# Three regroupings in a transformer-block kernel: order of the first loads, the last group's weight sums, and the first expert's W2

## The chip, the cores and the metric

The kernel runs on one core of one Trainium2 chip. The metric is the device time of one execution, in microseconds (us). Three runs of the kernel before gave 2044.21, 2045.13 and 2047.85 us; the median is 2045.13 us. TensorE is called PE here, VectorE DVE, ScalarE ACT, GpSimd POOL, SyncE SP, as in the profile.

## What is computed

One block of a perceiver over 16 batches of 128 query rows (`x`, 16 x 128 x 512) and 2048 context rows (`ctx`, 16 x 2048 x 512), all float32:

```python
x = x + xattn(layernorm(x), ctx, ctx, ...)      # 16 heads of 32, one shared K and V head
x = x + memory(layernorm(x), Ww, Wr, decay, log_alpha)   # chunks of 64, a 64x64 inverse per chunk and head
x = x + ffn(layernorm(x), Wg, w1, w2)           # 16 experts, top-1, capacity 128 rows each
```

Attention is softmax(Q K^T / sqrt(32)) V, then Wo. The memory layer projects v = x Ww^T, normalizes x per head to rk, inverts (I - A0) per chunk, forms the chunk's new values from v, reads them out with rk and projects with Wr^T. The FFN sends each row to the expert with the largest gate (at most 128 rows an expert, in order), computes relu(rows w1) w2 and multiplies by the gate.

## The kernel before

**Two stages.** `attention` does cross attention, the memory layer and the routing for 16 batches (b = 0 to 15, `LAST` = 15) and scatters each batch's rows to the dispatch table in DRAM. `experts` then takes the 16 experts one after the other, with the weights of the next one loaded meanwhile (two buffers of w1, two of w2, 4 MB each). Between the two stages all engines meet at the end of a block.

**The order of the work** is written out by hand. Every engine runs the same loop over batches and over 128 ticks a batch, and tables of ticks (`FIRST`, `SECOND`, `STEADY`, `PE_AT`, `ACT_AT`, `DVE_AT`, `POOL_AT`) say at which tick a step's instructions stand in that engine's program. So a tick sets only an order; waits on semaphores set the times. `prepare` makes batch b+1's queries, keys and values while batch b attends; `finish` runs batch b-1's projection, memory layer and routing in the same loop.

**Attention of a batch** has 4 groups of 4 heads. For each group PE computes the scores twice: once to find the row maxima on DVE (L425, `largest`), once transposed with the maximum subtracted (L438, `score`), 16 tiles of 128 keys. ACT exponentiates each tile into one of 18 buffers `p` (the tensor `weights`, L673). PE multiplies them with the values, four 32-column strips of the array at once (L450, `weigh`), and POOL adds the 16 tiles of a group elementwise into `psum` (even tiles) and `podd` (odd ones), L1053, and at the end the two into one, L1056 (`add_weights`). `sums` (L459 to L473) then sums over the 128 keys of the partitions with a matrix of ones, into KV_BANK, one strip of 32 output rows for each group, and adds up the outputs `oS` in P_BANK in the same way. DVE takes reciprocals (L900).

**The start.** SP loads the identity, Wq and the context chunks 1 to 3 of batch 0 (L329 to L332); ACT, at the head of its own program, loads the biases, x, Wk/Wv (`wkv`) and context chunk 0 (L662 to L665). Each of these two engines has a DMA queue of its own. PE projects chunk c with 8 matmuls of 32 columns (L507), in the order chunk 0, the transposes of x (L390), 4 filler matmuls (L642), chunk 1, the query projection (L492), chunk 2, the transposes of the first half of the keys and values, chunk 3, then the first scores (L425). The query, split into a high and a low part, is sent to its place by 12 small DMAs (`send_queries`, L340).

**The last batch** has nothing to run beside it: only its chain of dependent steps is left, from the last exponential to the scatter of its rows. PE is kept busy there with filler matmuls on zeros (`busy`, L454). The steps that the change touches, in PE's order: filler, `sums`, filler, the output projection `x1` in T_BANK, filler, transposes of xn2 (L390), filler, the four matmuls of the value projection V (L394 with `ww`), filler, transposes of rk, filler, rk times rk (`I`, L398), filler, transposes of XT (`X1`), and then six levels of the inverse. All but x1 go through P_BANK, and ACT copies each result out. `V` is first used after the inverse (`Vn`, L588).

**Counts.** Semaphores are counted by name: `Named` turns a step's name and its batch into the value to wait for, so a change of order needs a change of the names' order.

## Time and profile before

| | us |
|---|---|
| median of 3 runs (2044.21 to 2047.85) | 2045.13 |
| the profiled execution, its own time | 2050.84 |
| its span, first to last instruction | 2048.7 |
| PE busy in the span | 1978.4 (97%) |
| POOL busy | 1618.7 (79%) |
| DVE busy | 1287.9 (63%) |
| ACT busy | 1094.3 (53%) |
| mean granted PE clock | 0.982 of full |
| bytes moved by DMA | 262.21 MB, mean 128 GB/s |

Stages by the clock of the span: the first 160 us are a ramp in which PE has gaps; from there to about 1555 us batches follow one another; 1555 to 1622 us is the chain of the last batch; 1622 to 2048 us are the experts. A granted clock of 1.00 is the higher of PE's two levels (2.4 GHz), 0.50 the lower (1.2 GHz); a value between them is a stretch with some of each. PE's float32 matmuls are recorded as two instructions each, so x8 in a row of the trace is four matmuls of the program.

### The profile page before, as it was taken

The page shows a single profiled execution, that of the slowest core. Times are in us where ns is not written, and L with a number is a line of the kernel's source. Part 1 is how long each engine was busy: PE and PEld are TensorE (multiplying, and loading weights), DVE is VectorE, ACT ScalarE, POOL GpSimd, SP SyncE. Part 2 cuts the span into 40 slices and gives each one's busy share as a digit, 9 for nine tenths or more (in the row PEclk, how much of TensorE's full clock was granted, in tenths as well). Part 3 has the DMA queues.
Part 4 walks back from the last instruction along what each step waited for, and adds up shares of the span by engine and source line. Part 5 has one row for each costly group of instructions (what it writes and reads, how often), then busy time and mean ns, then how long its engine had stood idle before and what let it go on. Part 6 is the DMA issues. An engine that isn't in the chain of part 4 may idle for free. (4 is left out here: it accounts for less than half of the span.)

```text
span 2048.7 us, 34177 instructions
## 1 busy us (share of the span) xinstructions
PE 1978.4 (97%) x12396; PEld 1304.4 (64%) x12396; DVE 1287.9 (63%) x2218; ACT 1094.3 (53%) x2029; POOL 1618.7 (79%) x1387
## 2 busy tenths in 40 slices
PE   6889999999999999999999999999999899999998
PEld 3435565656565555556565556555556799999998
DVE  4776868677777768686877767686852333333333
ACT  2555665665656656666656566565553233333333
POOL 0778999998999999999999999999895155555555
PEclk7889999999999999999999999999999999999999
DMA  5434231212122221312121212211200399999994
GB/s 214 171 113 121 88 102 47 78 47 78 47 78 69 67 76 54 98 52 82 46 78 45 78 66 68 68 56 25 98 1 17 119 359 358 356 356 356 352 364 170
DMA packets 105127, 262.21 MB, mean 128 GB/s; under 512 B 8576, under 2 KB 33920, under 8 KB 96256
## 3 DMA queue, kind: packets, MB, share of 16 engines
q1 hardware_dynamic: 96336, 234.66, 33.2%
q10 hardware_dynamic: 5040, 14.88, 1.9%
q0 software_dynamic: 3584, 10.49, 1.3%
q8 instruction: 99, 1.62, 0.3%
q14 instruction: 68, 0.56, 0.1%
HBM read 223.67 MB, written 25.72 MB: 122 GB/s over the span
## 5 line engine op out<-in xcount | busy, mean ns | idle before, releaser
L848 DVE TENSOR_REDUCE mpart<-bank 128x1 f32<-128x512 f32 x1024 | 662.6, 682 | 239.2 <-PE bank L425 233.6
L673 ACT ACTIVATE weights<-bank 128x512 f32<-128x512 f32 x1024 | 581.9, 598 | 306.4 <-PE bank L438 304.7
L1053 POOL TENSOR_TENSOR podd<-podd,weights 128x512 f32<-128x512 f32 x384 | 495.1, 1289 | 32.5 <-ACT weights L673 31.6
L1053 POOL TENSOR_TENSOR psum<-psum,weights 128x512 f32<-128x512 f32 x384 | 503.6, 1311 | 2.6 <-ACT weights L673 1.6
L438 PE MATMUL bank<-qT,kT 97*128 97x512 f32 x1024 | 477.6, 473 | 5.7 <-DMA qT<-mrow 3.8
L425 PE MATMUL bank<-kT,qT 96*128 96x512 f32 x1024 | 426.5, 441 | 7.5 <-DVE mpart L848 5.9
L425 PEld LDWEIGHTS bank<-kT,qT 96*128 96x128 f32 x1024 | 195.5, 193 | 145.5 <-DVE mpart L848 110.9
L450 PE MATMUL bank<-weights,v 128*32 128x512 f32 x2048 | 274.8, 609 | 0.0
L438 PEld LDWEIGHTS bank<-qT,kT 97*128 97x128 f32 x1024 | 198.0, 194 | 110.0 <-ACT weights L673 51.1
L1309 POOL TENSOR_TENSOR w2l<-w,w2h 128x1024 fp32r<-128x1024 f32 x64 | 202.9, 3171 | 76.9 <-PE ebank L1222 56.1
L1252 ACT ACTIVATE hh<-ebank 128x512 fp32r<-128x512 f32 x64 | 38.2, 597 | 226.0 <-PE ebank L1206 226.0
L1246 ACT CAST w2h<-w 128x2048 fp32r<-128x2048 f32 x64 | 121.4, 1898 | 43.7 <-DMA w<-in_w 43.7
L507 PE MATMUL bank<-w_first,wkv 128*32 128x512 f32 x1024 | 127.1, 615 | 11.9 <-DMA w_first<-in_ctx 8.5
L1278 DVE SCALAR_TENSOR_TENSOR hl<-ebank,hh 128x512 fp32r<-128x512 f32 x64 | 44.2, 691 | 133.7 <-ACT hh L1252 133.7
L1273 DVE TENSOR_TENSOR w2l<-w,w2h 128x1024 fp32r<-128x1024 f32 x64 | 79.3, 1239 | 72.3 <-PE ebank L1222 49.6
L1206 PE MATMUL ebank<-dT,w_first 128*128 128x128 f32 x1024 | 118.3, 275 | 0.9 <-DVE dT L1267 0.9
L1206 PEld LDWEIGHTS ebank<-dT,w_first 128*128 128x128 f32 x1024 | 117.3, 192 | 2.4 <-issue 1.2
L1206 PEld LDWEIGHTS ebank<-dT,w 128*128 128x128 f32 x1024 | 117.5, 192 | 1.4
L1206 PE MATMUL ebank<-dT,w 128*128 128x128 f32 x1024 | 118.2, 275 | 0.0
L944 DVE TENSOR_TENSOR xr<-xr,bank 128x512 f32<-128x512 f32 (+2 forms) x114 | 62.9, 562 | 82.4 <-PE bank L398 80.1
L1220 PE MATMUL ebank<-w2h,hh 128*128 128x512 f32 x256 | 104.9, 410 | 1.9 <-POOL w2l L1309 1.9
L398 PEld LDWEIGHTS bank<-xr,Y 128*128 128x128 f32 x640 | 78.5, 191 | 43.4 <-DVE Y L930 30.8
(171 smaller groups left out, 2995.1 us busy)
## 6 DMA issues: line engine op xcount, KB each, us to landing
w<-in_w SPq DMA_DIRECT2D x48, 2048.0 KB, 20.1
w_first<-in_ctx SPq DMA_DIRECT2D x63, 1024.0 KB, 4.9
w_first<-in_w SPq DMA_DIRECT2D x16, 2048.0 KB, 11.7
dispatched<-route ACTq DMA_DIRECT2D x17, 513.0 KB, 4.2
dis<-dispatched SPq DMA_DIRECT2D x16, 513.0 KB, 3.5
qT<-qh SPq DMA_DIRECT2D x124, 64.0 KB, 2.1
qT<-qs SPq DMA_DIRECT2D x64, 64.0 KB, 2.1
xr<-in_x SPq DMA_DIRECT2D x16, 256.0 KB, 2.7
```

The lines of the kernel that those rows point to most:

```text
L425: e.matmul(a[:], qT[b % 2][0:3 * HD, (4 * g + h) * P:(4 * g + h + 1) * P], kT[b % 2][0:3 * HD, c * 512:(c + 1) * 512], start=True, stop=Tr ...
L438: e.matmul(B_BANK[u % 2][:], kT[b % 2][0:3 * HD + 1, k * P:(k + 1) * P], qT[b % 2][0:3 * HD + 1, g * 512:(g + 1) * 512], start=True, stop= ...
L450: ins = e.matmul(PV_BANK[HD * j:HD * (j + 1), :], v1[b % 2][:, k + j, :], p[(UNITS * b + u + j) % NP], start=k == 0, stop=k == KB - 4)
L507: ins = e.matmul(KV_BANK[row:row + HD, :], wkv[:, j, n:n + HD], cxT[c][:, j, :], start=j < 2, stop=j >= 2)
L673: e.activation(p[n % NP], B_BANK[u % 2][:], ACT.Exp).then_inc(p_act.sem, 1)
L848: e.tensor_reduce(mpart[g % 2][:, 4 * (n % 4) + n // 4:4 * (n % 4) + n // 4 + 1], max_bank(b, g, n)[:], AX.X, ALU.max).then_inc(max_dve.se ...
L1053: e.tensor_tensor(acc[:], first, p[(UNITS * b + u) % NP], ALU.add).then_inc(psum_pool.sem, 1)
L1206: ins = e.matmul(H_BANK[g][:, f * P:(f + 1) * P], w1[q][:, c, (4 * g + f) * P:(4 * g + f + 1) * P], dT[q][:, c, :], start=c == 0, stop=c = ...
L1220: e.matmul(Y_BANK[q][:], hh[g % 2][:, part], w2h[g][:, f, :], start=k == 0, stop=False)
L1246: e.copy(w2h[g][:], w2[q][:, 4 * g:4 * g + 4, :]).then_inc(w2h_act.sem, 1)
L1273: e.tensor_tensor(w2l[g % 2][:, 0:2, :], w2[x % 2][:, 4 * g:4 * g + 2, :], w2h[g][:, 0:2, :].bitcast(F32), ALU.subtract).then_inc(w2l_dve. ...
L1309: e.tensor_tensor(w2l[g % 2][:, 2:4, :], w2[q][:, 4 * g + 2:4 * g + 4, :], w2h[g][:, 2:4, :].bitcast(F32), ALU.subtract).then_inc(w2l_pool ...
```

## The change

Four edits.

1. **First loads.** SP now loads x, Wk/Wv, context chunk 0, Wq and chunks 1, 2, 3, in this order. ACT loads only the identity and the biases. In `FIRST`, batch 0's chunks 2 and 3 get earlier ticks, with the steps that follow from them, and the first row maximum too.
2. **Sums of the last group.** For the last batch's last group POOL adds only tiles 2 to 9 (`DIRECT` = 10). PE sums `psum`, `podd` and the six tiles 10 to 15 into the fourth strip of KV_BANK.
3. **Values of the last batch.** The V projection of the last batch moves behind `I` and goes to T_BANK; the transposes of rk no longer wait for it.
4. **W2 of expert 0.** The buffer `weights` becomes expert 0's (and every second expert's) w2 buffer; SP loads W2 of expert 0 as soon as `sums` of the last batch is done, in the attention stage, and no longer at the start of the expert stage.

```diff
-FIRST = Prep(norm=4, norm_pool=4, xn=6, xnt=8, xnt_act=8, qproj=[11, 12, 13, 40], q_dve=15, q_act=16, q_pool=18,
-             qsend=19, kv=[7, 10, 40, 62], kvlow=[7, 10, 16, 71], kvs=[8, 11, 17, 34], kh=[9, 12, 64, 89], kl=[11,
-             14, 51, 64], vt=[53, 67], vt_act=[76, 125])
+FIRST = Prep(norm=4, norm_pool=4, xn=6, xnt=8, xnt_act=8, qproj=[11, 12, 13, 14], q_dve=15, q_act=16, q_pool=18,
+             qsend=19, kv=[7, 10, 16, 18], kvlow=[7, 10, 16, 31], kvs=[8, 11, 17, 22], kh=[9, 12, 18, 37], kl=[11,
+             14, 20, 64], vt=[20, 67], vt_act=[20, 73])
+PE_LAST = dict(PE_AT, rkT=PE_AT["V"][0], I=PE_AT["V"][1], V=[PE_AT["X1"] - n for n in (4, 3, 2, 1)])
+ACT_LAST = dict(ACT_AT, rkT=ACT_AT["rk"] + 1, V=ACT_AT["X1"])
...
         @block.sync
-            e.dma_start(ident, T["consts"][:, C_IDENT, :]).then_inc(ident_in.sem, 16)
+            e.dma_start(xin[:], T["x"][0]).then_inc(x_in.sem, 16)
+            e.dma_start(wkv[:], T["Wkv"]).then_inc(wkv_in.sem, 16)
+            load_ctx(0, 0)
             weight(e, wq[:], "Wq").then_inc(wq_in.sem, 16)
             for c in (1, 2, 3):
                 load_ctx(0, c)
...
+                    if t == W2_AT and i == B:
+                        e.wait_ge(*sums_pe.at(LAST))
+                        for j in (0, 1):
+                            load_w2(e, T, weights, 0, j).then_inc(w2_in[j].sem, 16)
...
             def sums(b):
-                e.wait_ge(*psum_pool.at(b, 15 * HG - 1))
-                e.wait_ge(*oS_act.at(b, HG - 1))
+                e.wait_ge(*psum_pool.at(b, 15 * HG - 1 if b < LAST else 15 * (HG - 1) + DIRECT - 3))
+                if b < LAST:
+                    e.wait_ge(*oS_act.at(b, HG - 1))
...
+                sources = [[psum[(HG * b + g) % 5][:]] for g in range(HG)]
+                if b == LAST:
+                    sources[3] += [podd[:]] + [p[(UNITS * b + 3 * KB + k) % NP] for k in range(DIRECT, KB)]
+                for n in range(len(sources[3])):
+                    if b == LAST and n >= 2:
+                        e.wait_ge(*p_act.at(b, 3 * KB + DIRECT + n - 2))
                     for g in range(HG):
-                        ins = e.matmul(out[HD * g:HD * (g + 1), :], lhs, src[g][:], start=True, stop=True)
+                        if n < len(sources[g]):
+                            ins = e.matmul(KV_BANK[HD * g:HD * (g + 1), :], cst[:, C_ONES, 0:HD], sources[g][n],
+                                           start=n == 0, stop=n == len(sources[g]) - 1)
...
                 if t == PE_AT["rkT"]:
-                    e.wait_ge(*post_act.at(b, "V"))
+                    e.wait_ge(*post_act.at(b, "V" if b < LAST else "xn2T"))
                     e.wait_ge(*post_act.at(b, "rk3"))
...
         @block.scalar
+            e.dma_start(ident, T["consts"][:, C_IDENT, :]).then_inc(ident_in.sem, 16)
             e.dma_start(bias[:], T["bias"]).then_inc(bias_in.sem, 16)
-            e.dma_start(xin[:], T["x"][0]).then_inc(x_in.sem, 16)
-            e.dma_start(wkv[:], T["Wkv"]).then_inc(wkv_in.sem, 16)
-            e.dma_start(cxT[0], T["ctx"][0, 0]).then_inc(ctx_in[0].sem, 16)
...
             def add_weights(b, u):
-                if k < 2:
+                if k < 2 or (b == LAST and g == 3 and k >= DIRECT):
                     return
...
 def experts(nc, T, w1_first, w1_in_first, w2_first, w2_in_first):
-                    e.dma_start(w2[q][:, 8 * j:8 * j + 8, :], T["w2"][x].rearrange(
-                        "(h c p) m -> h p c m", p=P, h=2)[j]).then_inc(w2_in[q][j].sem, 16)
+                    if x:
+                        load_w2(e, T, w2[q], x, j).then_inc(w2_in[q][j].sem, 16)
```

How the instructions stand, at three places (the order of each engine's program, without times). First PE in the last batch, from the filler ahead of `sums` to the output projection (psum, podd, weights, oS: what is summed; mneg: the filler). Before:

```order
L457 MATMUL bank<-mneg 124x124 x8
L472 MATMUL bank<-psum,cst 32x512 x4
L472 MATMUL bank<-oS,cst 32x512 x4
L457 MATMUL bank<-mneg 124x124 x11
L394 MATMUL bank<-wo,turned 128x512
```

and with the change:

```order
L474 MATMUL bank<-mneg 124x124 x8
L495 MATMUL bank<-psum,cst 32x512 x4
L495 MATMUL bank<-podd,cst 32x512
L495 MATMUL bank<-weights,cst 32x512 x6
L500 MATMUL bank<-oS,cst 32x512 x4
L474 MATMUL bank<-mneg 124x124 x11
L411 MATMUL bank<-wo,turned 128x512
```

Seven matmuls are added, all for the fourth group, between those of `psum` and those of `oS`; the fillers on both sides stay.

Second, PE in the last batch from the transposes of xn2 to those of XT (ww: the V projection; rk: transposes; rkT: `I`; xr: XT). Before:

```order
L390 MATMUL bank<-cst,xn 128x128 x4
L457 MATMUL bank<-mneg 124x124 x4
L394 MATMUL bank<-ww,turned 128x512 x4
L457 MATMUL bank<-mneg 124x124 x4
L390 MATMUL bank<-cst,rk 128x128 x4
L457 MATMUL bank<-mneg 124x124 x4
L398 MATMUL bank<-rkT 128x128 x4
L457 MATMUL bank<-mneg 124x124 x12
L390 MATMUL bank<-cst,xr 128x128 x4
```

and with the change:

```order
L407 MATMUL bank<-cst,xn 128x128 x4
L474 MATMUL bank<-mneg 124x124 x4
L407 MATMUL bank<-cst,rk 128x128 x4
L474 MATMUL bank<-mneg 124x124 x4
L415 MATMUL bank<-rkT 128x128 x4
L474 MATMUL bank<-mneg 124x124 x4
L411 MATMUL bank<-ww,turned 128x512 x4
L474 MATMUL bank<-mneg 124x124 x12
L407 MATMUL bank<-cst,xr 128x128 x4
```

The V projection and its 4 fillers went from ahead of the transposes of rk to behind `I`, and the 12 fillers ahead of the transposes of XT stay.

Third, SP from the start of its program, with the change (w_first: a context chunk):

```order
L340 DMA xin<-in_x 128x512
L341 DMA wkv<-in_Wkv 128x256
L338 DMA w_first<-in_ctx 128x2048
L321 DMA wq<-in_Wq 128x2048
L338 DMA w_first<-in_ctx 128x2048 x3
L333 DMA xin<-in_x 128x512
L338 DMA w_first<-in_ctx 128x2048 x2
L324 DMA qT<-qh 32x4x128 x4
L324 DMA qT<-qs 32x4x128 x4
```

The identity left this queue for ACT's, and x, Wk/Wv and chunk 0 came to its head; from `xin<-in_x` of batch 1 on all stands as before.

## Rows read from the trace of the kernel before

**Rows 1.** Windows: two stretches, busy us (x instructions) by engine, clock, DMA share, GB/s.
```profile
600.00:1000.00 400.00, 395.65 (x2437) 232.88 (x2436) 298.73 (x533) 247.46 (x500) 367.70 (x342) 1.00 0.21 65
1700.00:1800.00 100.00, 100.00 (x708) 92.43 (x708) 35.25 (x43) 36.41 (x31) 58.24 (x24) 1.00 0.96 356
```

**Rows 2.** Timeline, PE, first 40 us: start, us, instruction, [idle before it <- releaser].
```profile
1.06 6.09 PE L385 MATMUL bank<-mneg 128*128 128x128 f32 x28 [1.06 <-DVE mneg L834]
15.65 3.64 PE L507 MATMUL bank<-w_first,wkv 128*32 128x512 f32 x16 [8.50 <-DMA w_first<-in_ctx]
...
21.25 1.92 PE L507 MATMUL bank<-w_first,wkv 128*32 128x512 f32 x16
24.71 3.81 PE L492 MATMUL bank<-xnT,wq 128*128 128x128 f32 x32 [1.54 <-issue]
...
34.16 3.54 PE L507 MATMUL bank<-w_first,wkv 128*32 128x512 f32 x16 [2.25 <-DVE kvs L877]
37.63 0.96 PE L425 MATMUL bank<-kT,qT 96*128 96x512 f32 x3
```

**Rows 3.** Windows of 2 us in the start: the last number is GB/s.
```profile
14.00:16.00 2.00, 0.35 (x4) 0.23 (x8) 0.00 (x0) 0.00 (x0) 0.00 (x0) 0.50 1.02 426
...
24.00:26.00 2.00, 1.29 (x11) 1.32 (x12) 1.36 (x3) 1.23 (x2) 0.00 (x0) 1.00 1.01 418
```

**Rows 4.** Timelines of DVE and SP in the start.
```profile
7.83 0.69 DVE L862 BATCH_NORM_STATS2 st<-xin 128x6 f32<-128x512 f32 x1 [2.24 <-DMA xin<-in_x]
...
32.96 2.54 SPq L313 DMA_DIRECT2D qT<-qs  x4
```

**Rows 5.** Timelines of PE, POOL and DVE at the end of the last batch's attention.
```profile
1555.08 1.97 PE L457 MATMUL bank<-mneg 128*124 128x124 f32 x16
1559.07 1.26 PE L472 MATMUL bank<-psum,cst 128*32 128x512 f32 x8 [2.02 <-POOL psum L1056]
1560.08 1.95 PE L472 MATMUL bank<-oS,cst 128*32 128x512 f32 x8
...
1568.27 1.03 PE L394 MATMUL bank<-wo,turned 128*128 128x512 f32 x2
...
1549.02 1.28 POOL L1053 TENSOR_TENSOR podd<-podd,weights 128x512 f32<-128x512 f32 x1
...
1562.08 0.96 DVE L900 RECIPROCAL x<-bank 128x128 f32<-128x128 f32 x1 [5.30 <-PE bank L472]
```

**Rows 6.** One microsecond there: the number before the last two is PE's clock.
```profile
1560.00:1561.00 1.00, 1.00 (x12) 0.22 (x4) 0.00 (x0) 0.00 (x0) 0.84 (x4) 0.50 0.06 16
```

**Rows 7.** Instructions of L450, 600 to 1000 us: ns min/median/max of one.
```profile
L450 PE MATMUL bank<-weights,v x552: 592/593/617, 601.5 to 998.1; 128*32 128x512 f32 x184
```

**Rows 8.** Timelines of PE and ACT in the last chain, V projection to X1.
```profile
1575.03 3.70 PE L394 MATMUL bank<-ww,turned 128*128 128x512 f32 x8
...
1580.77 1.13 PE L398 MATMUL bank<-rkT 128*128 128x128 f32 x8
1581.73 2.76 PE L457 MATMUL bank<-mneg 128*124 128x124 f32 x24
1584.33 0.60 PE L390 MATMUL bank<-cst,xr 128*128 128x128 f32 x4
...
1575.99 1.28 ACT L743 ACTIVATE rk<-xn,rn 128x128 f32<-128x128 f32 x4 [1.01 <-POOL rn L1087]
```

**Rows 9.** Timelines of PE, ACT and SP in the expert stage.
```profile
1628.91 7.38 PE L1206 MATMUL ebank<-dT,w_first 128*128 128x128 f32 x64 [0.88 <-DVE dT L1267]
1638.17 0.62 PE L1220 MATMUL ebank<-w2h,hh 128*128 128x512 f32 x1 [1.87 <-POOL w2l L1309]
...
1632.64 1.90 ACT L1246 CAST w2h<-w 128x2048 fp32r<-128x2048 f32 x1 [18.26 <-DMA w<-in_w]
...
1685.05 0.34 SPq L1171 DMA_DIRECT2D dis<-dispatched  x1
1710.74 0.34 SPq L1171 DMA_DIRECT2D dis<-dispatched  x1
```

More of the change, by code:

```diff
@@ L34 @@
 LEVELS = 6
+W2_AT = 20
+DIRECT = 10
 TICKS = 2 * UNITS
@@ L81, with __init__ @@
 class Named(Count):
-    def __init__(self, sem, names):
-        self.names = names.split()
+    def __init__(self, sem, names, last):
+        self.names, self.last = names.split(), (last or names).split()
         Count.__init__(self, sem, len(self.names))
     def at(self, n, name):
-        return Count.at(self, n, self.names.index(name))
+        return Count.at(self, n, (self.names if n < LAST else self.last).index(name))
 def groups_at(i, t, at):
@@ L128, in load_w1, with load_w2, attention @@
     return e.dma_start(dst[:, :, cols], T["w1"][expert].rearrange("(c p) f -> p c f", p=P)[:, :, cols])
-def attention(nc, T, w1_first, w1_in):
+def load_w2(e, T, dst, expert, half):
+    return e.dma_start(dst[:, 8 * half:8 * half + 8, :], T["w2"][expert].rearrange("(h c p) m -> h p c m", p=P, h=2)[half])
+def attention(nc, T, w1_first, w1_in, weights, w2_in):
     with ExitStack() as ctx:
@@ L167, in attention @@
         st1, mv1, rs1 = sb("st1", [P, 6]), sb("mv1", [P, 2]), sb("rs1", [P, 4])
-        weights = sb("weights", [P, NP * 512])
-        p = [weights[:, 512 * i:512 * (i + 1)] for i in range(NP)]
+        p = [weights[:, i, :] for i in range(NP)]
         oS, psum = [sb(f"oS{g}", [P, 512]) for g in range(HG)], [sb(f"psum{g}", [P, 512]) for g in range(HG + 1)]
@@ L468, in sums @@
                 e.wait_ge(*kv_read(b, ("s", 0)))
-                for out, lhs, src in ((KV_BANK, cst[:, C_ONES, 0:HD], [psum[(HG * b + g) % 5] for g in range(HG)]),
-                                      (P_BANK, cst[:, C_STACK, 0:HD], oS)):
-                    for g in range(HG):
-                        ins = e.matmul(out[HD * g:HD * (g + 1), :], lhs, src[g][:], start=True, stop=True)
+                sources = [[psum[(HG * b + g) % 5][:]] for g in range(HG)]
[4 more added lines that the diff above has]
+                        e.wait_ge(*p_act.at(b, 3 * KB + DIRECT + n - 2))
+                    for g in range(HG):
+                        if n < len(sources[g]):
+                            ins = e.matmul(KV_BANK[HD * g:HD * (g + 1), :], cst[:, C_ONES, 0:HD], sources[g][n],
+                                           start=n == 0, stop=n == len(sources[g]) - 1)
+                if b == LAST:
+                    e.wait_ge(*oS_act.at(b, HG - 1))
+                for g in range(HG):
+                    ins = e.matmul(P_BANK[HD * g:HD * (g + 1), :], cst[:, C_STACK, 0:HD], oS[g][:], start=True, stop=True)
                 ins.then_inc(sums_pe.sem, 1)
@@ L616, in finish @@
                     ins.then_inc(late_pe.sem, 1)
-                if t == PE_AT["loc"]:
+                if t == at["loc"]:
                     if b == LAST:
@@ L1125, in _, with experts @@
                         finish(i - 1, t)
-def experts(nc, T, w1_first, w1_in_first):
+def experts(nc, T, w1_first, w1_in_first, w2_first, w2_in_first):
     with ExitStack() as ctx:
@@ L1138, in experts @@
         w1 = [w1_first, sb("w11", [P, DC, F])]
-        w2 = [sb(f"w2{i}", [P, FT, D]) for i in range(2)]
+        w2 = [w2_first, sb("w21", [P, FT, D])]
         dis = [sb(f"dis{i}", [P, ROUTE]) for i in range(2)]
@@ L1154, in experts @@
         w1_in = [w1_in_first, [count(f"w1_in1{j}", 1, 16) for j in range(2)]]
-        w2_in = [[count(f"w2_in{i}{j}", 1, 16) for j in range(2)] for i in range(2)]
+        w2_in = [w2_in_first, [count(f"w2_in1{j}", 1, 16) for j in range(2)]]
         dT_pe, dT_dve = count("dT_pe"), count("dT_dve")
@@ L1325, in program @@
         w1_in = [Count(ctx.enter_context(nc.semaphore(f"w1_in0{j}")), 1, 16) for j in range(2)]
-        attention(nc, T, w1_first, w1_in)
-        experts(nc, T, w1_first, w1_in)
+        weights = ctx.enter_context(nc.sbuf_tensor("weights", [P, NP, D], F32))
+        w2_in = [Count(ctx.enter_context(nc.semaphore(f"w2_in0{j}")), 1, 16) for j in range(2)]
+        attention(nc, T, w1_first, w1_in, weights, w2_in)
+        experts(nc, T, w1_first, w1_in, weights, w2_in)
 def tables():
```

87 lines of the change are left out of this document (46 added, 41 removed).

## The prediction

> **What bounds the kernel now.** I read the windows by stage first. In the middle PE is busy for 395.65 of 400 us and in the expert stage for all of 100 us, both at the full clock [rows 1]. The change touches neither stretch: time can move only in the ramp at the start, in the chain of the last batch, and where the experts begin. So I then read PE's timeline in these three places, and at each gap what ended it.
>
> At the start PE has done its first fillers at 7.15 us (1.06 + 6.09) and waits 8.5 us for context chunk 0 [rows 2]. From there it is a chain: chunk 0, chunk 1, query projection, the sends, first scores at 37.63. In the last chain PE waits 2.02 us for POOL's sum of the last group [rows 5], and later only follows the others, with fillers between. In the expert stage there is one wait, 1.87 us before the first down projection, released by the split of W2 on POOL, which itself waited through ACT for the W2 load [rows 9].
>
> **Part 1, the first loads.** Before, two queues share the DMA engines, which together move 426 GB/s [rows 3], and chunk 0 stands third on its queue; its data is there at 15.65. A single queue is enough for that rate: from 24 to 26 us only SP's queue has loads, and 418 GB/s flow [rows 3]. In the new order, x (0.26 MB), Wk/Wv (0.13), chunk 0 (1.05), Wq (1.05) and chunk 1 (1.05) follow each other, with the identity (0.07) beside them. With a start near 2 us and a rate of 0.42 MB/us, chunk 0 (1.5 MB in all) lands near 6 us, Wq near 8.5, chunk 1 (3.6 MB) at about 11.0; I take 11.4 for the small packets ahead, and so the same end of all loads, near 16 us, as before.
>
> PE then goes: chunk 0 from 7.15 (1.92 us, as chunk 1 took) to 9.1. The transposes of x need x normalized. DVE's statistics started at 7.83 and waited for x [rows 4]; now x is there first and DVE is free 2.2 us earlier, so this is ready near 8.9. Four fillers, to 10.3. Chunk 1 starts when it lands, at 11.4, instead of at 21.25 [rows 2]: **9.8 us earlier**. Now PE waits there for the load, where before it was behind its own chain. The query projection needs Wq, which is long there, and ends 9.8 us earlier too (28.52 before, from 24.71 + 3.81). All behind it hangs on it: the split, then 12 sends, the last of SP's issued until 35.50 (32.96 + 2.54) [rows 4], the scores at 37.63.
>
> The new ticks of `FIRST` give little. Chunk 2 may not overwrite the bank before the query is read, and ACT issues four sends before it copies chunk 2 out, so chunk 3 starts at the same distance from the query projection as now (34.16, after a wait of 2.25 us, at 3.54 us instead of 1.92, so at the lower clock). The transposes of the first half now stand behind chunk 3, and ACT copies their result ahead of chunk 3's: 0.66 and 0.4 us more before the maxima; one DVE subtraction of 0.7 us goes behind them. Net **+0.4**. The first scores come at about 28.5. The loads of batch 1 queue behind those of batch 0, end near 21.5 and are before the sends. From there on every wait is on something that shifts as well, and the constants are loaded at ACT's ticks, so I let the shift reach the end of attention: **-9.4 us**.
>
> A rule speaks against this rate: by the Trainium skill ("DMA: Bandwidth & Descriptors", Specifications) a core's share of HBM ends at about 358 GB/s. With the page's figure, by estimate, the 3.6 MB up to chunk 1 would need 10.1 us, chunk 1 would land near 12.3, and this part would give about 8.5. This trace disagrees, with 418 and 426 in its rows, so the sum goes by the trace.
>
> **Part 2, the sums.** POOL's add of tile 9 ends at 1550.30 (1549.02 + 1.28) [rows 5], so PE no longer waits for POOL: after loc and 8 fillers it starts at 1557.05 (1555.08 + 1.97), not 1559.07: **-2.0**. Added are seven matmuls, all on one strip. A record on one of four strips lasts 592 ns at least [rows 7], while the eight of a round start within 1 us; eight of 592 do not fit in 1 us one behind another, so the strips run at once, and one alone saves nothing. The four matmuls of a round took 1.01 us (1559.07 to 1560.08) [rows 5], and the four full-width ones of V 3.70, with the end of the last, so some 0.9 each [rows 8]. I take 0.86: seven are **+6.0** (at 1.01 each 7.1; were a lone strip a quarter of a round, 1.8, which rows 7 exclude). What comes back: behind the old wait the clock is at 0.50 [rows 6], and the sums, two rounds, took 2.96 us (1559.07 to 1562.03) where two rounds at the full clock take 1.8: **-1.1**. DVE starts its reciprocals at 1565.0 instead of 1562.08 [rows 5]: +2.9. PE's 11 fillers after it run at the full clock now, where part of them was slow, so the last quarter of x1 (1568.27 before) starts at about 1570.5: **+2.2** for the chain.
>
> **Part 3, the values.** rk is ready at 1577.27 (1575.99 + 1.28) and was not waited for: V ran from 1575.03 to 1578.7, then the fillers, the transposes, and `I` at 1580.77 [rows 8]. Now the transposes can start at 1577.3 and `I`, after ACT's copy and the fillers (0.87), at 1578.8: 2.0 us earlier. But V goes to PE between `I` and X1, and PE has no room there. Before, X1 came at 1584.33, right behind 12 fillers (1581.73 to 1584.33, 2.60 us). Now behind `I` (ends 1579.8) stand 4 fillers (0.87), V (3.5) and the 12 fillers (2.6): X1 at 1586.7, **+2.4**.
>
> In addition PE now idles from 1575.0 to 1577.3, since V no longer fills the time until rk is there. Three waits of this length in this trace, 2.25, 2.02 and 1.87 us, are each followed by the lower clock: chunk 3's 3.54 us [rows 2], 0.50 [rows 6], and the slow stretch of expert 0, worked out in part 4. Chunk 3 lost 1.6 us by it. I take **+1.6**.
>
> **Part 4, W2.** SP issues it at about 1565 us; 4.2 MB take 10 us at 0.42 MB/us, and SP has only the last store and the experts' loads behind it. So W2 is there long before the experts. Before, ACT's first split waited for it until 1632.64 [rows 9]. The first down projection can follow the 64 records at 1636.3 (1628.91 + 7.38): the wait of 1.87 goes, and with it a slow stretch behind it. Its size: experts follow each other every 25.69 us (1685.05 to 1710.74 between the same loads). Expert 1's matmuls would end 2 x 25.69 behind 1628.91, so SP's load at 1685.05, which waits for them, comes 4.8 us later than that. About 1.0 of it is the reading out of the result; the rest is the wait of 1.87 and 1.9 us of slow matmuls behind it, whose first record lasts 0.62 us, more than one on two passes needs at the full clock [rows 7, 9]: **-3.8**. The later weights come 10 us earlier; PE does not wait for them now, so this gives nothing.
>
> **Sum.** -9.4 + 2.2 + 2.4 + 1.6 - 3.8 = **-7.0 us**. The profiled execution had 2050.84 us, so its like would have 2043.8; it stood 5.7 above the median of the runs, 2045.13, and against that I forecast **2038.1 us**.
>
> **Rivals.**
> (a) *The clock holds in the new gap before the transposes of rk.* Against it stand the three gaps above; for it, that the level after the 2.02 us fell only in the course of the next microsecond, so a gap just as long may miss it. The chain keeps 1.6 us: 2036.5.
> (b) *Lone strips count as little work*, and the clock falls during the seven matmuls. For it: no row has a lone strip, so nothing excludes it. Against it: PE is not idle there. Five of them at the lower level cost 5 x 0.85, and fillers of 2.4 us twice that until it recovers: up to 6, of which 1 to 2 hide in the reciprocals. With +4.5 the time is 2042.6, no change.
> (c) *One queue alone is slow at the start.* For it: the 418 were large chunks of context, while x and Wk/Wv at the head are small. If one queue carried only half of 426, chunk 1 would land at 18.9, and batch 1's x and two chunks, ahead of the sends on the same queue (8.1 MB in all), would hold the last sends until 40 us, where 37.6 was enough. The start would lose 2.8, the sum is +2.8 + 6.2 - 3.8 = +5.2: **slower, 2050.3**. It decides from a rate below about 220 GB/s; the row of 418 speaks against it.
> (d) *The early start is partly swallowed* in the ramp to 160 us, by a wait or a clock level that comes at another point. Half of it gone: 2042.8.
> (e) *The ramp gains beyond the shift*, since PE is denser at the start and misses a stretch at the lower level: 3 more us, 2035.
> (f) *The early W2 does not help*, since the rows of expert 0 or the split bind then: -3.2 in all, 2041.9.
>
> **How the numbers follow.** Forecast 0.47, (a) 0.15, (b) 0.10, (c) 0.04, (d) 0.10, (e) 0.09, (f) 0.05. A measurement of this kernel can tell about 0.2% from no change, 4.1 us; the border lies at 2041.0. Forecast, (a) and (e) lie below it; of the forecast's own spread (landing of chunk 1 within 1 us, clock within 2) a little crosses it, and of (b), (d) and (f) a third lies below. That makes 0.77 faster, 0.19 the same, 0.04 slower. The range reaches to (e) below with 2 us for the clock, 2033, and above past (b) and (d), 2043.5.
>
> **What would show it.** Right: the first score matmul near 28 us, chunk 1 at about 11.4; the sums of the last batch last 7 to 8 us on PE; from the first reciprocal to X1 it is about 25.5 us and not 22.3 (1562.08 to 1584.33); PE's wait before the first down projection is gone, and expert 0 takes 25.7 us. Wrong: a first score after 31 us (step 1), an end of the sums less than 2 us later (the seven matmuls overlap or are cheaper), X1 no later than before (a filler was on nobody's path), a new wait in expert 0. The whole would be wrong if the shift of the start is not found again at the start of the last batch.

## The result: 0.3% slower, and the profile after

The change was slower. Its median is 2053.2 us (20 runs, 2043.11 to 2059.83) beside 2045.25 for the kernel before (20 runs on the same chip); the ratio is 1.003, 95% interval 1.0019 to 1.0041. The forecast was 2038.1 us, and "slower" had 4 in 100.

One profile misleads here. The profiled execution of the change took 2043.11 us, the least of its 20, and read alone it agrees with the forecast: its span is 2041.0 us against 2048.7, a gain of 7.7 where 7.0 were forecast. So the lines of this one execution show whether the steps worked; what the typical execution loses has to be found elsewhere.

Busy time by engine, from the page of the profile after:

```profile
PE 1974.5 (97%) x12410; PEld 1300.9 (64%) x12410; DVE 1289.3 (63%) x2218; ACT 1094.4 (54%) x2029; POOL 1614.8 (79%) x1380
```

PE and POOL are 4 us less busy each than before; the mean granted clock is 0.989 (before 0.982), where the other 19 executions have 0.983 to 0.988.

Timeline of PE in the first 31 us, after (columns as in [rows 2]):

```profile
1.06 5.55 PE L402 MATMUL bank<-mneg 128*128 128x128 f32 x28 [1.06 <-DVE mneg L862]
9.62 3.30 PE L535 MATMUL bank<-w_first,wkv 128*32 128x512 f32 x16 [3.01 <-issue]
...
14.50 1.92 PE L535 MATMUL bank<-w_first,wkv 128*32 128x512 f32 x16
17.96 3.81 PE L520 MATMUL bank<-xnT,wq 128*128 128x128 f32 x32 [1.54 <-issue]
...
27.52 1.92 PE L535 MATMUL bank<-w_first,wkv 128*32 128x512 f32 x16 [2.95 <-DVE kvs L905]
...
30.33 0.98 PE L442 MATMUL bank<-kT,qT 96*128 96x512 f32 x3 [0.30 <-DMA qT<-qs]
```

Windows of 2 us there, after (the last number is GB/s, as in [rows 3]):

```profile
6.00:8.00 2.00, 0.61 (x6) 0.42 (x4) 0.65 (x4) 0.00 (x0) 0.95 (x3) 1.00 0.98 279
8.00:10.00 2.00, 0.38 (x4) 0.23 (x8) 0.00 (x0) 0.81 (x1) 0.00 (x0) 0.76 0.98 377
10.00:12.00 2.00, 2.00 (x12) 0.45 (x8) 0.00 (x0) 0.00 (x0) 0.00 (x0) 0.50 1.02 430
```

Chunk 0 starts at 9.62, not at 7.15: up to 8 us the transfers flow at 271 to 287 GB/s, and only later at 430. Behind that wait PE is at the lower clock (3.30 us for a chunk that takes 1.92). Chunk 1 starts at 14.50, where 11.4 was forecast and 21.25 stood before, and the first score at 30.33 instead of 37.63 [rows 2]: 7.3 us earlier. This start, too, belongs to one execution. g1_loads_w2, a kernel of the study below with the same loads, shows another, in its timeline of PE and its window from 6 to 8 us:

```profile
6.97 1.92 PE L520 MATMUL bank<-w_first,wkv 128*32 128x512 f32 x16
...
11.90 1.93 PE L520 MATMUL bank<-w_first,wkv 128*32 128x512 f32 x16 [1.46 <-DMA w_first<-in_ctx]
...
27.74 0.96 PE L438 MATMUL bank<-kT,qT 96*128 96x512 f32 x3 [0.31 <-DMA qT<-qs]
```

```profile
6.00:8.00 2.00, 2.00 (x19) 1.30 (x22) 0.65 (x4) 0.00 (x0) 0.95 (x3) 1.00 1.00 422
```

The same small transfers stand at the head of its queue, and yet 422 GB/s flow and chunk 0 starts at 6.97.

Timeline of PE in the last batch, after (answers to [rows 5] and [rows 8]):

```profile
1546.14 1.98 PE L474 MATMUL bank<-mneg 128*124 128x124 f32 x16
1548.05 1.07 PE L495 MATMUL bank<-psum,cst 128*32 128x512 f32 x8
1548.95 1.02 PE L495 MATMUL bank<-podd,cst 128*32 128x512 f32 x2
...
1555.91 2.65 PE L474 MATMUL bank<-mneg 128*124 128x124 f32 x22
...
1570.77 0.63 PE L407 MATMUL bank<-cst,rk 128*128 128x128 f32 x4 [2.48 <-ACT rk L771]
...
1572.10 1.13 PE L415 MATMUL bank<-rkT 128*128 128x128 f32 x8
1573.07 1.03 PE L474 MATMUL bank<-mneg 128*124 128x124 f32 x8
1573.93 3.60 PE L411 MATMUL bank<-ww,turned 128*128 128x512 f32 x8
1577.37 2.76 PE L474 MATMUL bank<-mneg 128*124 128x124 f32 x24
1579.97 0.60 PE L407 MATMUL bank<-cst,xr 128*128 128x128 f32 x4
```

The wait for POOL is gone, the sums take 7.9 us (1548.05 to 1555.91), the wait for rk is the new 2.48 us, and here the clock held in it (rival a): the 8 filler records behind it last 1.03 us, the full-clock size.

Timeline of PE at the first expert, after (answers to [rows 9]):

```profile
1624.86 7.38 PE L1234 MATMUL ebank<-dT,w_first 128*128 128x128 f32 x64 [0.88 <-DVE dT L1295]
1632.00 0.47 PE L1248 MATMUL ebank<-w2h,hh 128*128 128x512 f32 x1
```

The wait of 1.87 us before the first down projection is gone, as is the slow stretch behind it.

### The profile page after: what moved, and what is told of

It reads as the page before. It is cut to its first block and busy times, and to the rows that moved or that the text cites. A ratio compares the mean times of both kernels' runs of the same rounds, so it can differ in the third digit from the quotient of the medians.

```text
span 2041.0 us, 34191 instructions
## 1 busy us (share of the span) xinstructions
PE 1974.5 (97%) x12410; PEld 1300.9 (64%) x12410; DVE 1289.3 (63%) x2218; ACT 1094.4 (54%) x2029; POOL 1614.8 (79%) x1380
## 5 line engine op out<-in xcount | busy, mean ns | idle before, releaser
L1337 POOL TENSOR_TENSOR w2l<-weights,w2h 128x1024 fp32r<-128x1024 f32 x32 | 101.0, 3158 | 42.0 <-PE ebank L1250 27.5
L1337 POOL TENSOR_TENSOR w2l<-w,w2h 128x1024 fp32r<-128x1024 f32 x32 | 100.8, 3151 | 32.3 <-PE ebank L1250 27.7
L1343 POOL TENSOR_TENSOR pad<-pad 128x1 f32<-128x1 f32 x16 | 14.8, 924 | 109.6 <-issue 102.7
```

The source lines that it names most:

```text
L1337: e.tensor_tensor(w2l[g % 2][:, 2:4, :], w2[q][:, 4 * g + 2:4 * g + 4, :], w2h[g][:, 2:4, :].bitcast(F32), ALU.subtract).then_inc(w2l_pool ...
```

## The experiments

Sixteen kernels ran, in four groups of four; the kernels of a group and the runs of the kernel before ran on one chip. "Before" is its median in that group.

| label | kernel | us | before | ratio, 95% |
|---|---|---|---|---|
| e1_all | the change | 2053.68 | 2047.01 | 1.0028 (1.0016 to 1.0040) |
| e2_loads | before + first loads | 2040.31 | | 0.9966 (0.9954 to 0.9979) |
| e3_noloads | the change without first loads | 2058.31 | | 1.0055 (1.0037 to 1.0074) |
| e4_place | before + `weights` allocated first | 2055.81 | | 1.0042 (1.0027 to 1.0057) |
| e5_old_place | the change, `weights` at its old address | 2046.06 | 2048.05 | 0.9994 (0.9983 to 1.0005) |
| e6_align | e4_place, 1216 bytes further | 2046.06 | | 0.9990 (0.9979 to 1.0002) |
| e7_nohold | before, low keys written as zeros | 2028.95 | | 0.9905 (0.9873 to 0.9936) |
| e8_place_nohold | e4_place, low keys as zeros | 2027.93 | | 0.9912 (0.9878 to 0.9946) |
| g1_loads_w2 | first loads, early W2, aligned | 2035.88 | 2048.85 | 0.9947 (0.9930 to 0.9964) |
| g2_give_way | g1 + POOL gives way, 1 tick ahead | 2019.63 | | 0.9867 (0.9851 to 0.9884) |
| g3_give_way3 | g1 + POOL gives way, 3 ticks ahead | 2031.69 | | 0.9920 (0.9904 to 0.9936) |
| g4_sums | g1 + sums of the last group on PE | 2041.36 | | 0.9965 (0.9952 to 0.9979) |
| h1_all_give_way | the change + POOL gives way | 2029.45 | 2047.90 | 0.9910 (0.9897 to 0.9924) |
| h2_before_give_way | before + POOL gives way | 2032.69 | | 0.9927 (0.9914 to 0.9941) |
| h3_all_aligned_give_way | h1, aligned | 2027.04 | | 0.9902 (0.9888 to 0.9915) |
| h4_values | g1 + values later | 2040.01 | | 0.9964 (0.9952 to 0.9976) |

### Which edit loses: parts apart, and a fifth edit

To be loaded early, `weights` had to outlive the attention stage, so the change allocates it in `program`, ahead of all that `attention` allocates: it moved from byte 146752 of each partition to 49280, and what stood between moved up by its size. The prediction took this for free. e4_place makes only that move (W2 is still loaded in the expert stage):

```diff
         w1_first = ctx.enter_context(nc.sbuf_tensor("w1_first", [P, DC, F], F32))
+        weights = ctx.enter_context(nc.sbuf_tensor("weights", [P, NP, D], F32))
...
-        weights = sb("weights", [P, NP * 512])
```

e2_loads is the first edit alone, e3_noloads the other three with the old loads and the old `FIRST`.

> The changed kernel once more, to see in a second profile where the typical run (2053) loses against the profiled one (2043). Three theories. Placement: the weights buffer lies elsewhere in SBUF and every batch takes longer; then the time from batch to batch (94.34 us in the first profile, 94.23 before) is near 94.9 in a run of 2053. Phase: the new start sets another rhythm between the engines; the same sign, but only together with the loads. Clock: PE stays at the lower level for longer in the ramp or the last chain; then the batches in the middle keep 94.3 and the first 160 us or the last chain take some 8 us more.

> The kernel before with the new order of the first loads and the ticks of FIRST alone; weights buffer, sums, values and W2 as before. Placement theory: 9 to 10 us faster than before, about 2036. Phase theory: slow batches here too, so about 2045 to 2050. Clock in the ramp: no gain either. Clock or slow strips in the last chain: 2036.

> The changed kernel with the first loads and FIRST as before; sums, values, W2 and the moved buffer stay. By the traces the chain costs about 5.5 and expert 0 gives 3.8: 2047 if nothing else. Placement theory: 8 to 10 us more, about 2056. Phase theory and clock in the ramp: 2047.

> The kernel before with only the weights buffer allocated first, as in the change (W2 of expert 0 still loaded at the start of the expert stage). Placement theory: the batches take longer, 2053 or so in most runs. Phase and clock theories: no difference from before.

The loads gain 0.34%, 7 us. The placement alone loses 0.42%, 8.6 us. The residual load that SP issues once a batch gives the rhythm. Timeline of SP, these issues of batches 0, 4 and 13, kernel before:

```profile
146.11 0.43 SPq L366 DMA_DIRECT2D xr<-in_x  x1
...
523.00 0.43 SPq L366 DMA_DIRECT2D xr<-in_x  x1
...
1370.99 0.43 SPq L366 DMA_DIRECT2D xr<-in_x  x1
```

and e4_place:

```profile
149.07 0.43 SPq L365 DMA_DIRECT2D xr<-in_x  x1
...
525.80 0.43 SPq L365 DMA_DIRECT2D xr<-in_x  x1
...
1375.29 0.43 SPq L365 DMA_DIRECT2D xr<-in_x  x1
```

A batch takes 94.22 us before (9 of them from 523.00 to 1370.99) and 94.39 in e4_place. In the groups of POOL's instructions from 428 to 1370 us, the adds that read `weights` last longer, most of all those that read two tiles of it. Before:

```profile
L1053 POOL TENSOR_TENSOR psum<-weights 128x512 f32<-128x512 f32 x40 | 51.2, 1281 | 6.1 <-ACT weights L673 6.1
```

e4_place:

```profile
L1052 POOL TENSOR_TENSOR psum<-weights 128x512 f32<-128x512 f32 x40 | 52.3, 1308 | 6.0 <-ACT weights L672 6.0
```

That is 27 ns more for these adds (31 for podd<-weights, 12 and 6 where one operand is `podd` or `psum`), in an engine that is not the bottleneck. How such a thing can get to PE is seen in the one batch of e1_all that took 99.79 us (328.42 to 428.21 by the same issues; its neighbours took 94.36). Timeline of DVE there:

```profile
395.10 0.69 DVE L972 TENSOR_TENSOR xr<-xr,bank 128x512 f32<-128x512 f32 x1 [1.63 <-PE bank L415]
395.81 5.04 DVE L911 TENSOR_TENSOR kT<-kvs,kT 32x512 fp32r<-32x512 f32 x1
```

of POOL:

```profile
396.55 1.33 POOL L1081 TENSOR_TENSOR psum<-psum,weights 128x512 f32<-128x512 f32 x1
397.78 1.31 POOL L1081 TENSOR_TENSOR podd<-podd,weights 128x512 f32<-128x512 f32 x1
399.01 1.31 POOL L1081 TENSOR_TENSOR psum<-psum,weights 128x512 f32<-128x512 f32 x1
```

and of PE:

```profile
402.51 0.48 PE L447 MATMUL bank<-cst,mneg 128*128 128x128 f32 x1 [3.70 <-DVE mneg L883]
```

DVE's subtraction for the low part of the keys lasts 5.04 us and ends only when POOL's run of adds has ended (at 400.32 us); PE waits 3.70 us for the maxima behind it on DVE, and the next 8 us (402 to 410) are granted 0.58 of the clock. The kernel before has such records too. Its line in the trace (ns min/median/max of one):

```profile
L883 DVE TENSOR_TENSOR kT<-kvs,kT x64: 680/1196/7754, 24.6 to 1455.1; 32x512 fp32r<-32x512 f32 x64
```

and its longest record, in DVE's timeline, and then PE's wait behind it, in PE's:

```profile
113.66 7.75 DVE L883 TENSOR_TENSOR kT<-kvs,kT 32x512 fp32r<-32x512 f32 x1
```

```profile
123.07 0.47 PE L430 MATMUL bank<-cst,mneg 128*128 128x128 f32 x1 [5.20 <-DVE mneg L855]
```

e4_place has a second long one, in the same two timelines:

```profile
132.84 6.34 DVE L882 TENSOR_TENSOR kT<-kvs,kT 32x512 fp32r<-32x512 f32 x1
```

```profile
139.96 1.39 PE L424 MATMUL bank<-kT,qT 96*128 96x512 f32 x2 [6.37 <-DVE mpart L847]
```

Such a second long hold is not in every slow execution: in the profiles of the change (2043.11 us) and of e3_noloads (2056.20 us) the one near the start is the only record over 2.6 us. The regular part is small and the same in each batch. The longest record of the subtraction in a steady batch is 2.34 to 2.41 us before and 2.46 to 2.52 in e4_place, 0.12 of the 0.17 us that the batch gained; over the batches this makes about 2 of the 8.6 us. The rest is in the first 150 us or in a single long batch, at another place in each profile, and no record of a single execution adds it up. So the argument rests on the runs below that take the hold away, not on such a sum.

This gave the theory of the hold: in the batches this subtraction is DVE's one large instruction with both operands in SBUF, and while POOL's adds follow each other without a gap it does not get through. The Trainium skill has the rule ("SBUF — State Buffer", Who interferes with whom): such a DVE instruction contends with a GpSimd instruction that reads SBUF, and the one that comes second waits for the whole of the other. The trace agrees on the pair, but 7.75 us are six adds of 1.29, not one.

### Is it the address, and is it the hold?

> The change in full, but the weights buffer pinned to the address that it has in the kernel before (byte 146752 of each partition); all attention tensors then lie where they lay before. Placement theory (the time is lost because the adds of POOL on `weights` at its new address last some 25 ns longer): the 8.8 us of the placement come back, so about 2045, 2 us below the kernel before or the same; a batch takes 94.24 us, the adds psum<-weights 1281 ns. Rival (the address is innocent, what costs is that the buffer is shared with the experts or is loaded early): 2053 to 2054, like the change in full.

> The kernel before with the weights buffer ahead of the others as in the placement run, but 1216 bytes further on, so that it has the same offset modulo 2048 as the buffers psum and podd, as in the kernel before. If the relative alignment of an add's operands sets the 25 ns: adds of 1281 ns, 94.24 us a batch, time as before (2047). If the region of the memory sets it: adds of 1306 ns, 94.4 us a batch, 2055 to 2056.

e5_old_place pins the buffer to byte 146752 in both stages; every attention tensor then lies as before:

```diff
-        weights = ctx.enter_context(nc.sbuf_tensor("weights", [P, NP, D], F32))
+        weights = nc.alloc_sbuf_tensor_at("weights", [P, NP, D], F32, offset=146752)
```

It gives 0.9994, where the change in full had 1.0028. This run is not quite clean: to keep the address free its expert tensors stand in another order, and an expert takes 25.82 us in its trace where the change takes 25.69. Over 16 experts that is 2 us of its own, so the placement costs rather 9 us than 7 by this pair. e6_align allocates Wk/Wv, iota and four small tensors ahead of `weights`, which then begins at 50496 and not at 49280:

```diff
+        wkv = ctx.enter_context(nc.sbuf_tensor("wkv", [P, DC, 2 * HD], F32))
+        small = [ctx.enter_context(nc.sbuf_tensor(n, [P, s], F32)) for n, s in (("iota", E), ("decay", DH), (
+            "lalpha", DH), ("logg", DH), ("alpha", DH))]
         weights = ctx.enter_context(nc.sbuf_tensor("weights", [P, NP, D], F32))
```

Its group of adds, in the same stretch, is back at the old size, a batch at 94.24 us and the time at 0.9990:

```profile
L1049 POOL TENSOR_TENSOR psum<-weights 128x512 f32<-128x512 f32 x40 | 51.4, 1284 | 6.0 <-ACT weights L669 6.0
```

So it is not the region of the memory and not the sharing with the experts: a shift of 1216 bytes is worth 0.52% (+-0.19), some 10 us. (The constants and the projection matrices, which stand behind the buffer, shift by about as much; what changes in the trace is the length of the adds on `weights`.) At 50496 and at 146752 `weights` has the same offset modulo 2048 as `psum` and `podd` (1344), at 49280 it has 128. Three addresses fit that rule; they don't prove it.

The next pair takes the contention itself away. The low part of the keys is left out: DVE writes zeros in its place, so nothing is read from SBUF.

```diff
-                    e.tensor_tensor(kT[q][HD:2 * HD, ks], kvs[c // 2][keys(c), :], kT[q][keys(c), ks].bitcast(F32),
-                                    ALU.subtract).then_inc(kl_dve.sem, 1)
+                    e.memset(kT[q][HD:2 * HD, ks].bitcast(F32), 0.0).then_inc(kl_dve.sem, 1)
```

> The kernel before, with DVE's subtraction that makes the low part of the keys (two operands in SBUF, recorded at up to 7.75 us where 0.68 is the least) replaced by writing zeros there: the low part of the keys is left out. Theory of the hold (DVE's subtraction cannot start or finish while POOL adds back to back, and PE waits behind it): the long records of DVE vanish, the ramp to 160 us gets 3 to 6 us shorter, the whole 2041 to 2044. Rival (the long records lie beside other work): 2047, no change.

> The placement run with the same subtraction replaced. Theory of the hold: the 8.8 us that the placement costs are mostly holds that got longer or came at new points, so this comes out within 2 us of the same kernel with the old placement. Rival (POOL's longer adds cost by themselves, through the sums that PE waits for, or PE is hit directly): it stays 6 to 9 us above it.

Without the hold no cost of the placement is seen: 0.9905 and 0.9912, and 93.00 and 92.98 us a batch, though the adds psum<-weights still take 1309 ns in e8_place_nohold. With four runs each the two ratios are only good to 0.47% together, so their times alone would not exclude the 6 to 9 us of the rival; the batches agree with the theory, and the last group below has the sharper pair. The hold is far larger than was expected: the kernel before loses about 19 us to it (13 to 26 by the interval). In the profiles of before and of e7_nohold the last batch's residual load comes 21.0 us earlier: 9.3 of them stand already at batch 0's (146.11 to 136.83), the rest comes from batches of 93.0 us instead of 94.22. (A kernel below keeps the subtraction and has the same batch, so little of this is the shorter write.)

### A version that keeps the computation

If DVE cannot get between POOL's adds, POOL can step aside. Before the add that stands one tick ahead of the subtraction it waits until DVE has done it:

```diff
+                    for b, at in ((i + 1, t), (i + 2, t - TICKS)):
+                        if 1 <= b < B and at + 1 in prep(b).kl:
+                            e.wait_ge(*kl_dve.at(b, prep(b).kl.index(at + 1)))
                     if 0 <= i < B and t % 2:
                         add_weights(i, t // 2)
```

The base is g1_loads_w2: the two edits of the change that gain, the sums and values as before, the buffer at 50496. g4_sums adds the change's sums to it, h4_values (below) its moved values.

> The kernel before with two of the four edits, the order of the first loads and the early W2; the sums and the values of the last batch stay as before, and the shared buffer lies 1216 bytes further on than in the change (same offset modulo 2048 as psum). By the terms of the prediction (early W2 -3.8, loads 6.7 as measured alone): 10 us below the kernel before, about 2037; the last wait before expert 0's down projection gone. Rival: the early W2 gives nothing or is eaten by what follows (expert 0 bound by rows or by the split): 2040 to 2041, as the loads alone.

> The same, and POOL waits for DVE's subtraction (low part of the keys) before the add that stands one tick ahead of it, so that DVE is held for one add at most. Nothing is left out. Theory of the hold: the record of 7.75 us in the ramp becomes at most 2.5, a batch takes 93.0 to 93.5 instead of 94.25 us, and the whole comes out 12 to 19 us below the same kernel without the wait (writing zeros gave 19). Rival (POOL has no slack for it: its adds come late, and the sums and the weights' buffers with them): no gain, or slower than without.

> The same as the run before, but POOL stops three ticks ahead instead of one (one or two adds earlier). Theory of the hold: DVE is held less, but POOL idles longer, some 1 to 1.5 us at each of 4 places a batch of its 8 us of slack; within 3 us of the run before, either side. Rival as there.

> The kernel with the first loads, the early W2 and the aligned buffer, and in addition the change's sums of the last group on PE (seven lone-strip matmuls); the values stay as before. By the prediction's part 2: +2.2 us against the same kernel without. Rival (the PE that no longer waits keeps its clock, and what follows gains more than 1.1): 0 to -1. Rival on the other side (a lone strip lets the clock fall): +4.5 or more.

g2_give_way is the best kernel of the study: 2019.63 us, 1.33% below the kernel before and 0.8% below g1_loads_w2. Its line of the subtraction, and DVE and POOL in one batch:

```profile
L896 DVE TENSOR_TENSOR kT<-kvs,kT x64: 680/1046/4111, 15.3 to 1424.3; 32x512 fp32r<-32x512 f32 x64
```

```profile
570.08 1.15 DVE L896 TENSOR_TENSOR kT<-kvs,kT 32x512 fp32r<-32x512 f32 x1
...
569.38 1.30 POOL L1066 TENSOR_TENSOR podd<-podd,weights 128x512 f32<-128x512 f32 x1
571.30 1.28 POOL L1066 TENSOR_TENSOR psum<-psum,weights 128x512 f32<-128x512 f32 x1 [0.62 <-DVE kT L896]
```

POOL waits 0.62 us, DVE is held for the rest of one add only (1.15 us, where this place of a batch took 2.36 to 2.42 in g1_loads_w2), and PE's busy time in the window from 600 to 1000 us goes from 395.65 [rows 1] to 399.61:

```profile
600.00:1000.00 400.00, 399.61 (x2456) 233.72 (x2453) 295.51 (x537) 249.79 (x507) 368.32 (x347) 1.00 0.22 68
```

A batch takes 93.04 us. The expectation of "at most 2.5 us" in the ramp missed: there the longest is still 4.11, so the ramp has more to give. g3_give_way3 shows the price of stopping too soon: DVE is hardly held (median 682 ns), but POOL now waits for it. Its group of adds to podd, 428 to 1370 us:

```profile
L1066 POOL TENSOR_TENSOR podd<-podd,weights 128x512 f32<-128x512 f32 x242 | 308.6, 1275 | 21.3 <-DVE kT L896 21.3
```

A batch takes 93.71 us, and three quarters of the gain are gone (2031.69); the expectation (within 3 us) missed.

Whether the change itself lost only by the hold was left for the last group.

> The change in full at its own placement, with one edit more: POOL waits for DVE's subtraction before the add that stands one tick ahead of it (as in the run that gave 2019.6). If the loss of the placement works only through the holds: about 2019.6 + 3.9 (sums) + 2.4 to 3.9 (values) = 2026 to 2028, a batch at 93.0 to 93.1 us, and no difference to the same kernel with the aligned buffer. Rival (the longer adds cost by themselves): 8 us more than with the aligned buffer, 2034 to 2036.

> The kernel before with that wait alone. Theory: 16 us less than before (1.2 us at each of 14 batches less the slack, and what the ramp gets back), 2031 to 2034. Rival (the gain of the wait depends on the new first loads): under 8 us less.

> The change in full with the wait and with the shared buffer at the aligned place. Theory: within 2 us of the same kernel at the change's own place. Rival: 8 us less than it.

> First loads, early W2, aligned buffer and the moved value projection; the sums as before. It was 2035.9 without the values' move. By the prediction's part 3: +2.4 where the clock holds in the new gap before the transposes of rk, +4.0 where it falls, so 2038 to 2040; X1 at 38.1 to 39.7 us behind the last batch's residual load, where 35.8 without. Rival (the fillers are on nobody's path): 2036 and 35.8.

With POOL giving way the change comes to 2029.45 at its own place and to 2027.04 at the aligned one. Of the placement's 0.34 to 0.52% (e1 to e5, e4 to e6; +-0.16 and +-0.19) 0.08% is left, +-0.19. So most of the placement's loss does go once POOL gives way, and that it goes through the hold is shown to that accuracy. What is left is in the batches, 93.17 us against 93.04, as large as the difference of a batch without the wait: so what giving way took from the placement's loss lies outside this regular part. The expectations of h1 (2026 to 2028) and h3 (within 2 us of it) missed narrowly. The wait alone in the old kernel gives 0.73%, 15 us, as expected; between e1_all and h1_all_give_way it is 1.18%.

### The sums and the values alone

Measured from the last batch's residual load to X1, the chain took 35.75 us in g1_loads_w2 (1534.48 to 1570.23), 39.66 in g4_sums (1540.54 to 1580.20), 38.04 in h4_values (1536.18 to 1574.22). In g1_loads_w2 the timeline of PE at the sums reads:

```profile
1546.60 1.06 PE L485 MATMUL bank<-psum,cst 128*32 128x512 f32 x8 [2.02 <-POOL psum L1069]
1547.48 1.04 PE L485 MATMUL bank<-oS,cst 128*32 128x512 f32 x8
1548.46 2.65 PE L470 MATMUL bank<-mneg 128*124 128x124 f32 x22
```

The same wait of 2.02 us as in [rows 5], and the clock holds behind it: two rounds take 1.86 us, not 2.96. Of the eleven profiles with this wait the clock fell behind it in two, those of before and of e2_loads. The sums on PE cost 3.9 us in the chain (g4 against g1; 0.18% +-0.22 by the ratios, 5.5 us by the medians), which is 6.0 less 2.0 and nothing given back. The values cost 2.3 us where the clock held in the new gap (h4_values, h3_all_aligned_give_way, e1_all and the profiled execution of the change) and 3.8 to 3.9 where it fell (e3_noloads, e5_old_place, h1_all_give_way). Of e5_old_place here are the records behind the wait; against g4_sums its chain is 43.52 less 39.66 us:

```profile
1573.13 1.05 PE L410 MATMUL bank<-cst,rk 128*128 128x128 f32 x4 [2.49 <-ACT rk L774]
1573.97 1.86 PE L477 MATMUL bank<-mneg 128*124 128x124 f32 x8
```

## Why the prediction was wrong

Terms, in us, by ratios times 2048. By the intervals each has 2.6 to 4.4 us of uncertainty, so for sums, values and W2 the traces say more than the times; values, W2 and placement compare kernels of two groups:

| term | predicted | measured | from |
|---|---|---|---|
| first loads | -9.4 | -7.0 | e2_loads |
| sums | +2.2 | +3.7 | g4_sums less g1_loads_w2; chain +3.9 |
| values | +4.0 | +3.5 | h4_values less g1_loads_w2; chain +2.3, or +3.9 at the lower clock |
| early W2 | -3.8 | -3.9 | g1_loads_w2 less e2_loads; expert stage of the profiles -3.7 |
| placement of `weights` | none | +7.0 | e1_all less e5_old_place (+9 without that run's own 2 us) |
| sum | -7.0 | +3.3 | e1_all itself: +5.7; e5_old_place, without the placement, -1.2 |

**The failed step is a sentence of the opening, on what bounds the kernel**: "The change touches neither stretch: time can move only in the ramp at the start, in the chain of the last batch, and where the experts begin." It was read from the order of instructions, which indeed is unchanged there. The buffer's address is not in that order. It decides how long POOL's adds take (1281 or 1308 ns), and with that how long DVE's subtraction is held (at most 2.41 or 2.52 us in a steady batch, and longer holds besides). The placement, which the sum left at nothing without giving a reason, measured 7.0 us, or about 9. The prediction had neither the placement as a term nor a rival of this kind, so "slower" got 4 in 100, all of it for a slow queue (rival c), which did not happen: one queue carried 430 GB/s, and 250 at the least (e1_all, 4 to 6 us), above the 220 at which that rival began.

The placement is not the whole miss. Even without it the gain is not the forecast 7.0: the four measured terms make -3.7, and e5_old_place has -1.2 (+-2.3), or -3.2 without its slower experts. The first loads gave 2.4 us less than forecast and the sums cost 1.5 more. So without the placement, too, the gain would have been about half of the forecast or less. That the one profile of the change agreed so well (7.7 us for 7.0) was luck: it was the fastest of 20, set beside a profile of before that stood 5.7 above its median.

**Part 1** had the right mechanism, and its size came in some executions only. In g1_loads_w2 it went as written: chunk 0 at 6.97 us (7.15 forecast), chunk 1 at 11.90 behind a wait of 1.46 for its load (11.4), first score at 27.74 (28.5). In the change's profile the loads were slower up to 8 us, chunk 0 came at 9.62 and took 1.4 us more at the lower clock, and chunk 1 came right behind the fillers at 14.50. Over the eleven profiled executions with the new loads chunk 0 starts at 6.8 to 10.0 us and the first score at 27.7 to 31.3; why the rate in the first 8 us differs is open. So the term was sized from the good case: 9.4 us forecast, 7.0 (+-2.6) measured, and the prediction's own sign of being wrong, a first score after 31 us, is met in two of the eleven (31.23 and 31.31). The loads alone gained those 7.0 us over 11 runs, and in their profile the first score comes 6.8 us earlier (30.83): nothing of the shift was swallowed, so rival (d) fell. The 358 GB/s for a core's share of HBM that the Trainium skill gives ("DMA: Bandwidth & Descriptors", Specifications) did not bind: 414 to 434 GB/s flowed in g1_loads_w2 from 4 to 14 us. Rival (e), a ramp that gains beyond the shift, stays open: batch 0's residual load is issued at 133.01 to 139.59 us in seven profiled executions with the new loads, and at 139.85 to 149.07 in four with the old ones.

**Part 2** had the work right: seven matmuls at 0.86 each, the wait of 2.0 gone. The -1.1 for the clock, and the further 0.7 in the fillers, was read from a profile in which the clock fell behind that wait. In g1_loads_w2 it does not, and then there is nothing to give back. The same choice makes the whole comparison lean: the profiled execution of before reached X1 37.38 us after its last residual load (1546.95 to 1584.33), g1_loads_w2 35.75. Rival (b), lone strips that lower the clock, fell: 1.00 was granted from 1548 to 1556 us in the profile after.

**Part 3** was right: +2.4 for V and its fillers on PE's path, and 1.6 for the clock, which came in three of the seven profiles with this gap and not in the others.

**Part 4** was right in place and, as far as it can be told, in size: from the first expert's matmuls to the end it is 419.8 us in the profile before and 416.1 after. Part of that is the clock again; in e6_align, where it held behind a wait of 1.78 us, it is 418.3. Rival (f), nothing gained, fell.

What the prediction could have seen: the minimum and maximum of one line in the trace of before, 680 and 7754 ns for the same instruction on the same shape, and a wait of PE of 5.20 us behind it. It read the ramp only to its first 40 us. That the buffer's new address would lengthen the adds stood in no row of before.

## What to carry to other kernels

Before costing an edit, list what it moves in memory as well as in time, and look for the instructions of one shape whose longest record is many times the shortest: they are where a few nanoseconds elsewhere become microseconds. When an engine is held off by another's unbroken run, it is cheaper to let the other wait at a chosen point than to make either faster: three lines gave 0.7 to 1.2%, more than the two useful edits of the change together (0.53%). And with a spread of up to 17 us between executions of one kernel, take clock effects and the pace of the first loads from several profiles, never from one.

## What the runs showed of the hardware

- A DVE subtraction with both operands in SBUF (32x512, 0.68 us alone) was held for up to 7.75 us while POOL added back to back (1.29 us each): it did not get its turn at the boundary between two adds. Sometimes it did (1.15 to 2.4 us in the batches). What decides this is open.
- POOL's add of two tiles of `weights` into `psum` took 1281 to 1284 ns with the buffer at byte 146752 or 50496 of the partition, 1306 to 1309 ns at 49280.
- After a PE wait of 2.0 to 2.5 us the lower clock followed in some executions and not in others: behind the wait of 2.02 to 2.06 us for POOL's sum in 2 of 11 profiles ([rows 6] and e2_loads), behind that of 2.48 us for rk in 3 of 7 (e3_noloads, e5_old_place, h1_all_give_way).
- The same loads at the head of one queue flowed at 270 to 434 GB/s in the window from 6 to 8 us, depending on the execution (270 in e2_loads, 279 in the change's profile, 422 in g1_loads_w2, 434 in h4_values), and at 406 to 451 GB/s from 10 to 14 us. Why is open.
